# Splitting all matmul weights into two parts at an even rate in the first stage of a two-block graph network

## What is computed

```python
h = jnp.maximum(_layernorm(x, axis=-1), 0.0)
x = x + _L0_gnn_ref(h, adj, ...)      # W_proj, 8 heads, leaky_relu, mask, softmax, relu
h = jnp.maximum(_layernorm(x, axis=-1), 0.0)
x = x + _L1_gnn_ref(h, adj, ...)      # 3 layers:
    mask = adjacency_matrix.astype(jnp.float32) + jnp.eye(n) > 0
    scores = leaky(si[:, :, None] + sj[:, None, :] + attn_b[l]); scores = where(mask, scores, -inf)
    agg = softmax(scores) @ x;  h = layernorm(x + agg, g1[l], beta1[l])
    ff = gelu(h @ W1[l] + b1[l]) @ W2[l] + b2[l];  x = layernorm(h + ff, g2[l], beta2[l])
```

## Time and profile before

| what | value |
| --- | --- |
| median of three runs | 1514.67 us |
| profiled execution, own time | 1514.97 us |
| its span, first to last instruction | 1513.2 us |
| TensorE busy (matmuls) | 1464.8 us, 97% |
| VectorE, ScalarE, GpSimd busy | 1366.1, 1161.8, 904.2 us |

### The profile page before, as it was taken

How to read it: one execution, slowest core, us unless ns; L and a number is a source line. 1 busy time by engine, 2 the same in 40 slices (tenths; PEclk the granted TensorE clock), 3 DMA queues, 4 the chain that set the end, 5 groups by cost and what they waited for, 6 DMA issues and landing times.

```text
span 1513.2 us, 35107 instructions
## 1 busy us (share of the span) xinstructions
PE 1464.8 (97%) x11264; PEld 1242.7 (82%) x11264; DVE 1366.1 (90%) x4311; ACT 1161.8 (77%) x2042; POOL 904.2 (60%) x1006
## 2 busy tenths in 40 slices
PE   6899999499999999999999999999999999999997
PEld 3677777388888888888888888888888888888886
DVE  7999999898989899989898999898989998989864
ACT  5788888468787878787777777777777777777784
POOL 5799998336364647564645566545555665555465
PEclk9999999699999999999999999999999999999999
DMA  6543433610000112110011121100011220000001
GB/s 200 153 153 125 136 126 115 175 38 15 8 15 24 34 35 78 48 32 8 15 26 32 39 74 51 28 8 15 26 32 49 64 64 15 9 15 8 15 29 56
DMA packets 70891, 82.78 MB, mean 55 GB/s; under 512 B 29281, under 2 KB 54113, under 8 KB 70753
## 3 DMA queue, kind: packets, MB, share of 16 engines
q1 hardware_dynamic: 69120, 74.76, 17.0%
q0 software_dynamic: 816, 3.15, 0.6%
q10 hardware_dynamic: 816, 3.15, 0.5%
HBM read 38.95 MB, written 25.17 MB: 42 GB/s over the span
## 4 chain that ended last, share of the span: by engine, by line
PE 93%; DVE 4%; issue 1%; POOL 0%; DMA 0%; ACT 0%; SPq 0%; DVEq 0%; ACTq 0%; POOLq 0%
PE bank L765 36%; PE bank L789 36%; PE bank L357 3%; PE bank L746 3%; PE bank L347 3%; PE bank L755 3%; PE bank L315 2%; PE bank L345 2%; PE bank L332 2%; PE bank L325 1%; PE bank L342 1%; PE bank L734 1%; DVE w_lo L575 0%; PE bank L726 0%; DVE shifted L552 0%
## 5 line engine op out<-in xcount | busy, mean ns | idle before, releaser
L789 PE MATMUL bank<-w_hi,hid_hi 128*128 128x256 f32 x1528 | 428.1, 280 | 1.3 <-DVE hid_lo L1028 1.3
L789 PE MATMUL bank<-w_hi,hid_lo 128*128 128x256 f32 x1528 | 427.2, 280 | 0.0
L789 PE MATMUL bank<-w_lo,hid_hi 128*128 128x256 f32 x1528 | 426.7, 279 | 0.0
L844 ACT ACTIVATE bank<-bank,b_col 128x512 f32<-128x512 f32 x384 | 251.8, 656 | 196.1 <-PE bank L765 195.2
L765 PE MATMUL bank<-nT_hi,w_hi 128*128 128x512 f32 x768 | 317.3, 413 | 1.6 <-DVE nT_lo L1157 1.6
L1028 DVE TENSOR_TENSOR hid_lo<-bank,hid_hi 128x512 fp32r<-128x512 f32 x384 | 259.5, 683 | 60.7 <-ACT hid_hi L849 58.8
L765 PE MATMUL bank<-nT_hi,w_lo 128*128 128x512 f32 x768 | 304.6, 397 | 0.0
L765 PE MATMUL bank<-nT_lo,w_hi 128*128 128x512 f32 x768 | 304.0, 396 | 0.0
L789 PEld LDWEIGHTS bank<-w_hi,hid_hi 128*128 128x128 f32 x1528 | 286.7, 188 | 15.2 <-DVE hid_lo L1028 1.7
L789 PEld LDWEIGHTS bank<-w_lo,hid_hi 128*128 128x128 f32 x1528 | 286.3, 187 | 13.1
L789 PEld LDWEIGHTS bank<-w_hi,hid_lo 128*128 128x128 f32 x1528 | 287.1, 188 | 0.0
(11 more groups left out here) (137 smaller groups left out, 3127.3 us busy)
## 6 DMA issues: line engine op xcount, KB each, us to landing
raw_weights<-xin SPq DMA_DIRECT2D x96, 128.0 KB, 2.3
xin<-in_x_dram SPq DMA_DIRECT2D x16, 512.0 KB, 4.0
first_block_out<-x_res SPq DMA_DIRECT2D x16, 512.0 KB, 2.7
second_block_in<-x_act SPq DMA_DIRECT2D x16, 512.0 KB, 3.7
xin<-second_block_in SPq DMA_DIRECT2D x16, 512.0 KB, 3.9
x_fin<-first_block_out SPq DMA_DIRECT2D x16, 512.0 KB, 4.0
out_dram<-x_fin SPq DMA_DIRECT2D x15, 512.0 KB, 2.9
xh_other<-xh SPq DMA_DIRECT2D x128, 33.0 KB, 2.1
```

The source lines that it names most:

```text
L789: mm = pe.matmul(FF[t // 2][:, (t % 2) * D:(t % 2 + 1) * D], a[:, r, t * P:(t + 1) * P], w[:, l, c, :], start=(c == 0 and t % 2 == 0 and p ...
L844: act.activation(h[:], h[:], ACT.Gelu, bias=b1_col[:, l, c:c + 1]).then_inc(s_gelu, 1)
```

## The change

- `HEAD` becomes 28 and the loop ends at step 59 (`LOOP_END` 60), so steps 12 to 27 and 60 to 63 are written out. There are 48 split steps, 12 to 59; each splits 256 columns (`WP`): ScalarE makes the `hi` piece, GpSimd the `lo` piece, at the places in the step where the W2 pieces were. VectorE splits no weights.
- The `lo` parts get memory of their own (`first_lo`, `later_lo`), the raw weights too (`raw`, `later_raw`). They are loaded in 12 DMAs of 512 KB, issued by ScalarE at steps 3, 4, 6, 8 and 10, 12, ... 24. GpSimd issues no DMA. ScalarE waits at step 12 for the first four and at step 27 for the other eight.
- `make_mask` on VectorE goes. GpSimd adds the diagonal to the integer adjacency in place (`add_loops`): at steps 66, 69 and 72, and at the end of a slot for slot s+3. ScalarE turns it into 1e30 for no edge and 0 for an edge (`make_mask`, Relu of 1e30 - 1e30*a): at steps 68 and 72 and after `high` 1 of a slot for slot s+2. `scores` subtracts it and waits for `s_mask`.
- Masks are made only for layer 0 in both.

```diff
-            HEAD, LAG = 16, 10
-            W1_PARTS = {6: (0, 1), 7: (2, 3), 8: (4, 5), 9: (6, 7), 10: (8, 9), 11: (10,), 12: (11,)}
+            HEAD, LOOP_END, LAG = 28, 60, 10
+            W_AT = LOOP_END - WN
...
+            def load_weights(eng, dst, l, kind, half, done):
+                src, rows = ((w1, KD), (w2, CF))[kind]
+                cs = slice(half * rows // 2, (half + 1) * rows // 2)
+                eng.dma_start(dst.rearrange("p (c f) -> p c f", c=rows)[:, cs],
+                              src[l].rearrange("(c p) f -> p c f", p=P)[:, cs]).then_inc(done, 16)
...
 first_scalar:
-                        for l in range(L):
-                            act.dma_start(raw[:, l].rearrange("p (c f) -> p c f", c=KD),
-                                          w1[l].rearrange("(c p) f -> p c f", p=P)).then_inc(s_w1[l], 16)
-                    for part in w1_parts(tau):
-                        act.wait_ge(s_w1[l], 16)
-                        act.copy(w1_part(w1_hi, part), raw[:, l, q * W1P:(q + 1) * W1P]).then_inc(s_whi, 1)
+                    for n, at in enumerate((3, 4, 6, 8)):
+                        if isinstance(tau, int) and tau == at:
+                            load_weights(act, raw[:, n // 2], 0, n // 2, n % 2, s_wraw)
+                    for n in range(4 * (L - 1)):
+                        if isinstance(tau, int) and tau == 10 + 2 * n:
+                            l, kind = n // 4, n // 2 % 2
+                            load_weights(act, later_raw[:, l, kind], l + 1, kind, n % 2, s_later)
...
-                    if splits_w2(tau):
-                        act.copy(w2_part(w2_hi, tau), raw_part(tau)).then_inc(s_whi, 1)
+                    if splits(tau):
+                        source, hi, lo = split_part(tau)
+                        act.copy(hi, source).then_inc(s_whi, 1)
 first_gpsimd:
-                    if splits_w2(tau):
-                        pool.wait_ge(s_whi, 4 * L + 1 + (tau - HEAD))
-                        pool.tensor_tensor(w2_part(w2_lo, tau), raw_part(tau),
-                                           w2_part(w2_hi, tau).bitcast(F32), ALU.subtract).then_inc(s_w2lo, 1)
+                    if splits(tau):
+                        pool.wait_ge(s_whi, tau - W_AT + 1)
+                        pool.tensor_tensor(lo, source, hi.bitcast(F32), ALU.subtract).then_inc(s_wlo, 1)
-                        pool.wait_ge(s_wlo, 4 * (l + 1))
-                        pool.dma_start(raw[:, l].rearrange("p (c d) -> p c d", c=CF),
-                                       w2[l].rearrange("(c p) d -> p c d", p=P)).then_inc(s_w2, 16)
 first_vector:
-                    for part in w1_parts(tau):
-                        dve.tensor_tensor(w1_part(w1_lo, part), raw[:, l, q * W1P:(q + 1) * W1P],
-                                          w1_part(w1_hi, part).bitcast(F32), ALU.subtract).then_inc(s_wlo, 1)
 second part:
+                    pool.tensor_tensor(adj_raw[:, g], adj_raw[:, g], node_int[:].unsqueeze(1).broadcast_to([P, TG, N]),
+                                       ALU.add).then_inc(s_edges, 1)
+                    act.activation(mask[:, g].rearrange("p t j -> p (t j)"), adj_raw[:, g].rearrange("p t j -> p (t j)"),
+                                   ACT.Relu, bias=far[:], scale=NEG).then_inc(s_mask, 1)
-                        score.done(dve.tensor_tensor(mask_sum, adj_raw[:, g], node_of[:].unsqueeze(1).broadcast_to([P, TG, N]),
-                                                     ALU.add))
-                        score.done(dve.tensor_scalar(mask[:, g], mask_sum, 0.0, NEG, ALU.is_le, ALU.mult))
```

More of the change, by code:

```diff
@@ L151, in graph_net @@
         with first:
+            later_raw = sb("later_raw", [P, L - 1, 2, W], where=first)
             wcat = sb("wcat", [P, KD, WC], where=first)
             batt_row = sb("batt_row", [P, H], where=first)
-            s_w1 = [sem(f"w1_loaded{l}") for l in range(L)]
-            s_w2, s_ready = sem("w2_loaded"), sem("w2_seen")
+            s_wraw, s_later = sem("first_layer_weights_loaded"), sem("later_weights_loaded")
             s_col, s_rows, s_cat, s_batt = sem("columns_loaded"), sem("rows_loaded"), sem("wcat_loaded"), sem("batt_loaded")
@@ L206, in steps @@
                     step(tau, tau)
-                with eng.Fori(HEAD // 4, NT // 4) as i:
+                with eng.Fori(HEAD // 4, LOOP_END // 4) as i:
                     for t in range(4):
                         step(i * 4 + t, t)
+                for tau in range(LOOP_END, NT):
+                    step(tau, tau)
                 for tau in range(NT, NT + LAG):
@@ L571, in step, with w1_of, w2_of @@
                                           ALU.subtract).then_inc(q_asd, 1)
-                    for part in w1_parts(tau):
-                        l, q = part // 4, part % 4
-                        dve.wait_ge(s_whi, part + 1)
-                        dve.tensor_tensor(w1_part(w1_lo, part), raw[:, l, q * W1P:(q + 1) * W1P],
-                                          w1_part(w1_hi, part).bitcast(F32), ALU.subtract).then_inc(s_wlo, 1)
                 steps(dve, step, tail)
         with second:
+            later_lo = sb("later_lo", [P, L - 1, 2, W], F32R, where=second)
+            def w1_of(w):
+                return w.rearrange("p (c f) -> p c f", c=KD)
+            def w2_of(w):
+                return w.rearrange("p (c d) -> p c d", c=CF)
+            w1_hi, w2_hi = [w1_of(w_hi[:, l, 0]) for l in range(L)], [w2_of(w_hi[:, l, 1]) for l in range(L)]
+            w1_lo = [w1_of(first_lo[:, 0])] + [w1_of(later_lo[:, l, 0]) for l in range(L - 1)]
+            w2_lo = [w2_of(first_lo[:, 1])] + [w2_of(later_lo[:, l, 1]) for l in range(L - 1)]
             nT_hi, nT_lo = (sb(n, [P, 2, KD, TOK], F32R, where=second) for n in ("nT_hi", "nT_lo"))
@@ L787, in output @@
                     for t in range(TG):
-                        for p, (a, w) in enumerate(((hid_hi, w2_hi), (hid_hi, w2_lo), (hid_lo, w2_hi))):
+                        for p, (a, w) in enumerate(((hid_hi, w2_hi[l]), (hid_hi, w2_lo[l]), (hid_lo, w2_hi[l]))):
                             mm = pe.matmul(FF[t // 2][:, (t % 2) * D:(t % 2 + 1) * D], a[:, r, t * P:(t + 1) * P],
-                                           w[:, l, c, :], start=(c == 0 and t % 2 == 0 and p == 0),
+                                           w[:, c, :], start=(c == 0 and t % 2 == 0 and p == 0),
                                            stop=(c == CF - 1 and p == 2), skip_group_check=True)
@@ L1002, in some, with tail @@
                             post(i, s - 1)
+                        if nxt3 and layer_group(s + 3)[0] == 0:
+                            add_loops(i, s + 3)
+                def tail(tau):
+                    if tau == NT + 2:
+                        pool.wait_ge(q_loops, 2)
+                        add_loops(0, 0)
+                    if tau == NT + 5:
+                        add_loops(0, 1)
+                    if tau == NT + 8:
+                        add_loops(0, 2)
                 def after(U):
```

113 lines of the change are left out of this document (59 added, 54 removed).

## The result

Nine runs of the changed kernel have a median of **1517.87 us** (1516.22 to 1524.75), nine of the kernel before, beside them, 1514.12 (1513.37 to 1514.86). The ratio is 1.0033, interval 1.0025 to 1.0042: **slower by 0.33%**, where I had forecast 8.2 us less. (The ratio goes by all runs, whose means are 1519.33 and 1514.08; the medians are 3.75 us apart.) The runs also lie 8.5 us apart, those of before 1.5. The profiled one is the slowest, 1524.75 us with a span of 1522.3, so its trace shows more loss than the median has.

A forecast was written before the change was run, and what follows sets the result against it. TensorE was taken to set the pace in the loop and second part, but not in the fill. Terms -10.2 + 0.7 + 3.0 - 0.5 - 1.2 = -8.2 us gave 1506.5 beside the median, range 1502.5 to 1512.0.

The forecast's parts named there:

- Term 1: Fill before the loop: VectorE's weight pieces and GpSimd's three DMAs leave it; gain 10.2 us, between 7.0 and 10.8.
- Term 2: Written-out steps 12 to 27: ScalarE's DMA issues make `w_hi` late for GpSimd; loss 0.7 us, between 0 and 3.7.
- Term 3: Split steps: GpSimd's longer `w_lo` piece blocks VectorE's `shifted`; 0.094 us in each of 32 loop steps, 3.0 lost.
- the ring: Waits in a split step from `shifted` to `x_res` to `w_lo` and back: 3.94 us in the loop, 3.81 written out.
- the sign: In loop steps of the profile after, `shifted` would take about 0.9 us, ending some 0.6 us after `w_lo` ends.
- The loop term of 3.0: The 32 loop steps take 3.94 us against TensorE's 3.846, so 3.0 us lost.
- steps 12 to 27 at no cost: Written-out split steps have a ring of 3.81 us, so they stay with TensorE's pace and lose nothing.
- rival B: The lock costs its full length: loop steps 4.09 us, written-out steps 3.96, 1513.1 in all; chance 0.12.
- Term 4: Passage, steps 64 to 73: VectorE's mask leaving gains 1.2 us, GpSimd's addition loses 0.7; gain 0.5.
- Term 5: Slot 0: without VectorE's mask `hid_lo` comes earlier and TensorE's 1.29 us wait goes; gain 1.2, between 0 and 1.3.
- Term 6: All later slots: TensorE is the bound; 13 other masks on ScalarE and additions on GpSimd fit idle time, costing nothing.

The follow-up runs named there:

- the trace without such a wait: The changed kernel with its masks on VectorE again, weights as changed: 1514.96 us against 1514.61, ratio 1.0015.

## Why the prediction was wrong

*Term 1, the fill: right.* Forecast -10.2, measured -9.9 from the first `scored` to that of step 16, in both traces. By its own sign, `leaky` of tile 0 to that of tile 8, the forecast was 29.2 us and the trace has 29.9.

*Term 2, loads issued by ScalarE: the wrong cost.* I asked what an issue costs ScalarE, and its 0.35 to 0.45 us cost nothing, nor did the larger piece. What I left out is the transfer. The change adds 4 MB of loads to steps 10 to 24, beside 1 MB of stores every four steps, and the two that were waited for in the trace were needed 3.7 and 4.5 us after their issue; the earlier trace rows show no wait for a store, and so I took the resource to be free. In the profiled run that gave 6.1 us of waits and 1.45 us of half clock behind the longer one, 7.2 net against the trace without such a wait, and in all runs most of the spread. With the loads between the stores 2.0 were left, of stores that were late for another reason. The Trainium skill, "DMA: Bandwidth & Descriptors", section Issuing engines are not separate DMA queues, says it in a sentence: transfers from ScalarE's and SyncE's queues run on the same 16 engines and interleave. The runs agree: 5.8 us for the store with the load beside it, 4.0 with the load 1.5 us behind it. I had not drawn on it.

*Term 3, the lock: right in kind, too small by 0.15 us a step.* Forecast 3.94 in the loop and 3.81 written out, measured 4.09 and 3.935. The step that failed is the walk round the ring, from `w_lo` straight to `shifted`. Between them on VectorE stand `neg` and `vare`, and `neg` is blocked by the piece (0.60 us with the piece of 256 columns, 0.19 at the median with that of 128), so that it ends with the piece and `vare` comes only then. The 0.15 us that I took off for what a blocked `shifted` has already done, and for overlap, isn't there: `shifted` takes 0.68 us, not the 0.9 that I had named as the sign. The loop term of 3.0 became 7.8, and "steps 12 to 27 at no cost" became 12 x 0.09 = 1.1. So rival B, the lock at its full length, is what happened to this term: it had 4.09 and 3.96, without naming `neg`, and I gave it 0.12. The Trainium skill, "SBUF — State Buffer", section SBUF: two separate sides, counts VectorE's two-port modes among what locks, not only instructions with two SBUF inputs; I had read the second half only. `neg` is a one-input instruction of two columns and could fall only under the first; no row shows the mode it ran in, but that it waits for the piece's end the rows above show. With the measured 8.9 us in place of 3.0 the forecast would have been 1512.4, so this term alone doesn't reach the measured time.

*The loop's own cost* isn't in the forecast as a term: my 1.38 of the earlier trace rows for the loop against 1.25 of the earlier trace rows did contain it (0.13, measured 0.155), and with the ring under TensorE's pace it was free. Once the ring was the bound it cost 5 us.

*Term 4, the passage: wrong in sign*, 0.5 gained by forecast; it lost 0.8, and 0.6 with the shorter steps 60 to 68 (0.2) counted. *Term 5, slot 0: right*, 1.3 gained.

*Term 6, "all later slots: nothing": wrong by 5 us.* I set the additions against 528 us of GpSimd's idle time, although I had just argued from the earlier trace rows that what counts is with what an instruction of GpSimd coincides. 0.72 us in the wrong place moved 5.4 us of GpSimd's work into VectorE's products and cost 1.04 us a lap boundary, 3.1 in all; put in the gap it cost 0.2 us over all later slots (1149.38 against 1149.14). The other 2.1 us (32 slots x 0.065) are the place of tensors in memory, which nothing in the profile of before could show.

The sum by these figures, against the kernel before: fill -9.9, an earlier first step -0.9, late stores in steps 17 to 28 +2.0 and the ring there +1.2, loop +7.8, a shorter end of the first part -0.2, passage +0.8, slot 0 -1.3, lap boundaries +3.1, place +2.1: +4.7, where the run with loads between the stores, from which the first of them are taken, was profiled at 1518.22, 3.25 more than before. The difference is slot 0's opening, 14.01 us before and 12.76 in that run, and 1.4 us of it is the clock, which was at 0.50 for 5.95 and 3.10 us of it. With that the sum is +3.3. I had no term for the clock. The changed kernel and that run have the same second part and yet 5.02 and 3.10 us of it, so it says nothing about the change.

## What to carry to other kernels

Count an idle gap of GpSimd or VectorE only after you have seen what the other one does in it: list all instructions around it that can be blocked, the tiny ones too, and add the whole length of the new one to the ring. The same additions of 0.72 us cost 3.1 us together in one place and 0.2 in another.

New transfers are priced by what lands in the same microseconds, not by the issue. Look for the buffer ring with the least slack, read from its store's issue to the instruction that needs the slot (here 3.7 to 5.0 us at the waits, where such a store took 3.7 us at best), and issue in the phase where its store isn't in flight. If runs that lay within 1.5 us now lie 8 apart, look for such a collision first: moving eight loads by one or two steps brought the spread back to 1.9.

Before you give a residue between two traces to the change, take each stretch's granted clock and the start of its first piece of work out of it: here these were up to 1.5 and 2.1 us between traces.

A gain in one stage vanishes if the same change slows the next one past the bound: the pieces that left the fill, 9.3 us once, came back as 0.25 us in each of 32 steps, 7.8 in all.

## What I had not expected of the hardware

- A two-column `tensor_scalar` of VectorE, 0.12 to 0.22 us before, takes 0.60 when GpSimd's 0.73 us instruction has begun ahead of it, and 0.55 when that is one of 228 columns.
- The same instructions in a hardware loop on the engines need 0.155 us more a step than written out (4.09 against 3.935), when VectorE and GpSimd wait for each other.
- Matmuls that stream 256 columns of fp32r from one tensor took 285 ns, and 280 after that tensor was moved by 8208 bytes in each partition; moving `nT_hi` with it made slots of layer 0 0.15 us shorter (24.91 against 25.06). Which property of the address matters is open.
- A late store can be partly free: after a stall of 4.3 us five steps ran at TensorE's 3.85 before the ring took hold again at 3.94, 0.45 us given back.
- It can also cost more than its wait: after TensorE had idled 4.11 us, its granted clock was 0.50 from 68.16 to 71.58 us, and the next step took 1.45 us more than TensorE's pace. Not every stall does it: of the four waits of 3.7 to 4.3 us in the traces three were followed by such a fall, of the shorter ones none.
